# Per-token maxima of an adapter moved from a double PSUM bank to a ring of single banks, in two-head pieces

## What is computed

```python
end_pos = encoder_hidden_states.shape[1] - NUM_TOKENS        # 508 keys, 4 tokens
enc, ca = encoder_hidden_states[:, :end_pos], encoder_hidden_states[:, end_pos:]
hs = _mha(hidden_states @ Wq, enc @ Wk, enc @ Wv)            # 8 heads of 20
ca_q1 = jnp.einsum('btc,th->bch', ca, Wq_ca)                 # 96 queries
ca_q1 = ca_q1[:, indices, :]                                 # spread over the 256 rows
ca_hs1 = _mha(ca_q1, residual, residual)                     # the token scores
ca_hs2 = _mha(ca_hs1 @ Wq, ca @ Wk_ca, ca @ Wv_ca)
out = (hs + ca_hs2) @ Wout + b_out + residual
```

## Time and profile before

| | us |
|---|---|
| median of 3 runs | 1375.84 (1375.4 to 1378.92) |
| the profiled execution | 1376.87 |
| its span in the trace | 1375.0 |
| TensorE busy | 1272.2 (93%) |
| VectorE busy | 963.3 (70%) |
| GpSimd busy | 810.6 (59%) |
| ScalarE busy | 779.5 (57%) |

### The profile page before, as it was taken

How to read it: one execution, slowest core, us unless ns; L and a number is a source line. 1 busy time by engine, 2 the same in 40 slices (tenths; PEclk the granted TensorE clock), 3 DMA queues, 4 the chain that set the end, 5 groups by cost and what they waited for, 6 DMA issues and landing times. The chain is left out here.

```text
span 1375.0 us, 39629 instructions
## 1 busy us (share of the span) xinstructions
PE 1272.2 (93%) x16812; PEld 1084.5 (79%) x16812; DVE 963.3 (70%) x1758; ACT 779.5 (57%) x1420; POOL 810.6 (59%) x866
## 2 busy tenths in 40 slices
PE   4889999976999999999889999999999999999597
PEld 3677777755989989899757888888888888887597
DVE  4677887734777777777457767686867676765584
ACT  2366666644656665665346656565656665655364
POOL 2278887657645655555426656566656565667364
PEclk9999999957999999999969999999999999999798
DMA  6001110002000000000010000000010000000000
GB/s 133 21 11 50 50 35 2 2 7 65 2 2 2 2 3 2 2 2 2 1 42 8 2 8 2 8 2 8 1 49 2 2 2 2 2 2 2 13 15 25
DMA packets 31992, 20.40 MB, mean 15 GB/s; under 512 B 21415, under 2 KB 30347, under 8 KB 31819
## 3 DMA queue, kind: packets, MB, share of 16 engines
q1 hardware_dynamic: 31819, 17.88, 5.2%
HBM read 16.56 MB, written 1.31 MB: 13 GB/s over the span
## 5 line engine op out<-in xcount | busy, mean ns | idle before, releaser
L530 POOL TENSOR_TENSOR cross_probs_l<-cross_probs 128x1024 f16<-128x1024 f32 x160 | 302.6, 1893 | 54.6 <-ACT cross_probs L614 54.6
L614 ACT ACTIVATE cross_probs<-cross_score 128x1024 f32<-128x1024 f32 x160 | 163.9, 1024 | 189.4 <-PE cross_score L844 189.4
L698 DVE TENSOR_REDUCE cross_top<-cross_max 128x2 f32<-128x1024 f32 x160 | 195.7, 1223 | 63.6 <-PE cross_max L818 63.6
L1618 POOL TENSOR_TENSOR ad_probs_l<-ad_probs 128x1024 f16<-128x1024 f32 x64 | 120.8, 1893 | 91.2 <-ACT ad_probs L1692 90.8
L530 POOL TENSOR_TENSOR self_probs_l<-self_probs 128x1024 f16<-128x1024 f32 x80 | 151.4, 1892 | 1.2 <-ACT self_probs L614 1.2
L864 PEld LDWEIGHTS cross_pv<-cross_v_h,cross_probs 128*128 128x128 bf16 x1280 | 117.1, 98 | 38.0 <-issue 26.8
L614 ACT ACTIVATE self_probs<-self_score 128x1024 f32<-128x1024 f32 x80 | 81.9, 1024 | 110.9 <-PE self_score L844 110.8
L864 PE MATMUL cross_pv<-cross_v_h,cross_probs 128*128 128x65 bf16 x1280 | 135.7, 196 | 6.1 <-POOL cross_probs_l L530 5.3
L865 PE MATMUL cross_pv<-cross_v_l,cross_probs 128*128 128x64 f16 x1280 | 134.4, 194 | 0.0
L866 PE MATMUL cross_pv<-cross_v_h,cross_probs_l 128*128 128x65 bf16 x1280 | 134.0, 194 | 0.0
L844 PE MATMUL cross_score<-cross_qk_h 64*128 64x256 f32 x640 | 120.5, 373 | 0.0
(11 more groups left out here) (438 smaller groups left out, 4792.4 us busy)
## 6 DMA issues: line engine op xcount, KB each, us to landing
ad_ctx_rows<-in_ctx SPq DMA_DIRECT2D x8, 192.0 KB, 2.8
cross_ctx_rows<-in_ctx SPq DMA_DIRECT2D x8, 192.0 KB, 2.6
sw_raw<-in_L_xattn_wq SPq DMA_DIRECT2D x2, 640.0 KB, 6.1
sw_raw<-in_L_xattn_wk SPq DMA_DIRECT2D x2, 640.0 KB, 4.8
sw_raw<-in_L_xattn_wv SPq DMA_DIRECT2D x2, 640.0 KB, 5.2
cw_raw<-in_L_xattn_wq SPq DMA_DIRECT2D x2, 640.0 KB, 4.2
lr_raw<-in_L_xattn_w_ff SPq DMA_DIRECT2D x2, 640.0 KB
out<-x_rows SPq DMA_DIRECT2D x8, 160.0 KB, 1.9
```

The source lines that it names most:

```text
L530: nc.gpsimd.tensor_tensor(probs_l[:, n % PR, :, :].rearrange("p j k -> p (j k)"), whole, whole.bitcast(BF16)[:, 1::2], ALU.subtract).then_ ...
L614: nc.scalar.activation(probs[:, n % PR, :, :].rearrange("p j k -> p (j k)"), score_bank[:, :], ACT.Exp, scale=SCALE).then_inc(exped, 1)
L698: nc.vector.reduce_max(out, scores, AX.X).then_inc(max_read, 1)
L1618: nc.gpsimd.tensor_tensor(probs_l[:, n % PR, :, :].rearrange("p j k -> p (j k)"), whole, whole.bitcast(BF16)[:, 1::2], ALU.subtract).then_ ...
```

## The change

The maxima of the token scores (`top`) go through the shared banks. A group is two heads instead of four: 2 x 256 columns fill one bank. Four groups of a batch stand in pairs at the ends of the slots `4b+1` and `4b+2`, and VectorE reduces each with one instruction of 512 columns. `top` now has its place in the ring, so a batch has four more entries and the banks of all later entries are dealt out anew. The two semaphores of their own go. Besides, `qs`, the token scores, stand behind the second half of weigh in the step instead of before it.

```diff
         add(1, "xv", 4)
+        if (p := pair(g, WEIGH)) is not None:
+            out += [(1, ("weigh", p, group)) for group in (2, 3)]
         add(1, "qs", 4, 0)
         add(1, "qs", 5, 1)
-        if (p := pair(g, WEIGH)) is not None:
-            out += [(1, ("weigh", p, group)) for group in (2, 3)]
-        add(1, "top", 1, 0)
-        add(1, "top", 2, 1)
+        for n in range(4):
+            add(1, "top", 1 + n // 2, n)
         add(1, "rows", 0)
...
-    ELSEWHERE = ("weigh", "top", "qs", "s2", "p2", "xv")
+    ELSEWHERE = ("weigh", "qs", "s2", "p2", "xv")
...
                             _, b, n = key
-                            dve.wait_ge(top_filled, b * 2 + n + 1)
-                            nc.vector.reduce_max(top_q[:, CDIM + 4 * n:CDIM + 4 * n + 4],
-                                                 max_bank[0:CDIM, :].rearrange("p (h k) -> p h k", h=4), AX.X).then_inc(top_read, 1)
+                            dve.wait_ge(filled, order.filled(key))
+                            nc.vector.reduce_max(top_q[:, CDIM + 2 * n:CDIM + 2 * n + 2],
+                                                 shared[order.bank(key)][0:CDIM, :].rearrange("p (h k) -> p h k", h=2), AX.X).then_inc(emptied, 1)
...
                 elif what == "mq":
-                    pe.wait_ge(top_read, b * 2 + 2)
+                    pe.wait_ge(emptied, order.read(("top", b, 3)))
...
                     pe.wait_ge(emptied, order.read(("k", p)))
-                    after(pe, top_read, extra_fills(g, 1))
                 after(pe, max_read, p * ROUNDS + step)
...
-            def top(g, b, n):
+            def top(b, n):
 
                 j = b % 2
                 if n == 0:
                     pe.wait_ge(emptied, order.read(("rows", b)))
                     pe.wait_ge(cm_ready, b + 1)
-                after(pe, top_read, b * 2 + n)
-                after(pe, max_read, issued(g, MAX))
-                for h in range(4):
-                    mm = nc.tensor.matmul(max_bank[0:CDIM, h * SEQ:(h + 1) * SEQ], c_m[j][0:3 * HT, 4 * n + h, :],
+                bank_ = claim(("top", b, n))
+                for h in two:
+                    mm = nc.tensor.matmul(bank_[0:CDIM, h * SEQ:(h + 1) * SEQ], c_m[j][0:3 * HT, 2 * n + h, :],
                                           r_s[j][0:3 * HT, :], start=True, stop=True)
-                mm.then_inc(top_filled, 1)
+                mm.then_inc(filled, 1)
```

## The result

| | before | after |
|---|---|---|
| median of 20 runs each, us | 1377.38 | 1372.03 |
| ratio, 95% interval | | 0.9958 (0.9941 to 0.9975) |
| profiled execution, us | 1376.87 | 1368.42 |
| its span, us | 1375.0 | 1366.6 |

The change makes the kernel faster, by 5.8 us as the ratio has it (3.4 to 8.1). The ratio leaves out one slow run on each side, 1591.92 us before and 1389.86 us after. The forecast was 10.8 us: the sign and the range of 1357 to 1374 us were right, the size was about double. The time also lies outside the 1361 to 1371 us that the forecast gave to its own case. The profiled execution does not show where the missing half went: its adapter is 10.9 us shorter (last value matmul at 289.46 us for 300.34), close to the 11.4 that the sum gave.

The account below looks back on a forecast made before the run. TensorE, busy 93% of the span, was taken as the bound, with idle time and half clock in the adapter. Start 2.1, six batches 3.6, last batch 3.0, tail 1.2 + 1.5 sum to 11.4 us: forecast 1365 us, range 1357 to 1374.

Parts of the forecast that it names:

- its own case: The forecast's main case for the whole kernel: 1365 us, within 1361 to 1371 us, chance 0.50.
- (g): Clock in six steady batches: one in three falls after the x wait, 1.5 us worse; 0.6 us each, 3.6 us.
- (f): Last batch: no x in slot 30, so no new wait; 3.7 us if the clock stays up, 3.0 taken.
- (h): Tail: with slot 32's wait halved, the clock falls later or not at all; 1.5 us, between 0 and 6.
- (d): Token scores behind the values: shorter waits for ScalarE's exponential of the scores; 1.2 us from slots 32 and 33.
- (a): Top leaves the double bank: in slot 17 find_max goes at 162.35 us instead of 163.72.
- (b): VectorE's maximum split into two of 512 columns: +0.07 to +0.15 us a pair, 1.1 to 2.4 us in all.
- (c): Slots 17 and 18: VectorE is late next, TensorE waits 1.2 to 1.4 us at x; 1.1 us gained for the batch.
- (e): Start: slots 2 and 3 lose waits of 1.41 and 1.36 us, less the split pair; 2.1 us gained.
- slower rival: Falls after x last twice as long, costing each of six batches 2.1 us: 1386 us, chance 0.07.
- rival with a fall in every batch: The clock's fall merely moves to uncovered work in every batch: 2.4 us gained, about 1374 us, chance 0.15.

Follow-up runs that it names:

- x_first: Kernel after, with x ahead of mt in the ring and mt behind the first half of weigh: 1361.92 us, 0.9878 of the kernel before.
- only_top: Kernel after, with the token scores put back ahead of the values, so only the maxima move: 1365.54 us, 0.9921 of the kernel before.
- only_qs: Kernel before, with only the token scores moved behind the values, the maxima left in the double bank: 1379.35 us, 1.002 of the kernel before.
- before_b: Kernel before, no edit, executed for its second profile: span 1376.7 us.
- the last version: Kernel after, with x ahead of mt and the token scores back ahead of the values: 1360.91 us (0.9876), later 1357.84 us (0.9869).
- after_b: Kernel after, no edit, executed again for its third profile: median 1370.12 us, 0.9945 of the kernel before, span 1380.0 us.
- after_d: Kernel after, no edit, executed for its fifth profile: span 1362.1 us.

## Where the prediction was right, and the steps that failed

The step that failed is the clock, in (g) and with it in (f) and (h); (d) failed besides. The waits of (a), (b) and (c) came out nearly as forecast. The marks that split the adapter are the first value matmul, the first `ot` transposes of slots 9, 29 and 33, and the last value matmul. In us gained, five columns against the first profile of before, and last the mean of the five profiles after against the mean of the three before:

| term | forecast | after, 1 | after, 2 | after, 3 | after, 4 | after, 5 | means |
|---|---|---|---|---|---|---|---|
| start (e) | 2.1 | 2.8 | 2.9 | -0.9 | 3.1 | 2.3 | 3.3 |
| first steady batch | 0.6 | 2.8 | 2.8 | 2.8 | 2.8 | 2.8 | 1.7 |
| next five (g) | 3.0 | 5.7 | 1.8 | -9.2 | 5.7 | 0.2 | 1.2 |
| last batch (f) | 3.0 | -0.4 | 3.4 | 4.2 | -1.2 | 4.2 | 0.3 |
| tail (d, h) | 2.7 | 0.0 | 0.0 | 1.5 | 0.0 | 1.2 | 0.5 |
| sum | 11.4 | 10.9 | 10.9 | -1.7 | 10.4 | 10.7 | 7.0 |

(a) and (b) were right for `find_max`, which follows at once, and for the split pair, 1.28 us. The split costs 0.07 us a pair, the lower bound of the sum and under the 0.125 us of its estimate. But `top` 1 is "about to issue when its bank comes free" in slot 17 and not in every batch; in slots 9, 21 and 25 it waits 0.6 us for the reading of q, which the sum had at nothing. The prediction had named this wait as a sign of being wrong. Its share was not measured by itself either.

(c) was right: VectorE is next, the wait at `x` is 1.1 to 1.25 us, and a batch without a fall is 1.0 to 1.2 us shorter than one of before with its short fall. x_first shows it from the other side: with the bank of `x` free earlier, VectorE's 1.2 us of idle and 0.8 us of the batch go. I missed the new wait of `qw` for k, 0.37 us; its share was not measured by itself.

(d) was wrong by its 1.2 us. The guard was in the text, that the exponential of the token scores has only 0.2 us to spare, but it was read off slot 17, where the token scores do not wait. In slots 32 and 33 they wait for ScalarE in either order, and their exponential starts 0.62 us behind them in both kernels (slot 32). The values no longer stand between it and the next scores to cover it: these wait 0.44 us with `find_max` in between, and 0.95 us behind slot 33, where there is no `find_max`. only_top and only_qs say the same: the move brings nothing that can be measured.

(h) had 1.5 us, and the profiles have none in three cases and 1.5 and 1.2 us in two. The clock of the tail was down from 268 us on with the wait halved, as from 277 us before; in the third and fifth profile it fell 7 to 8 us behind the start of the token scores of slot 32 (289.2 and 275.9 us), not 1 to 2 us as in the first two, and those are the ones that gained.

(f) was read off one profile. Its 3.0 us rest mostly on the fall of 6.8 us in slot 30, and the other two profiles of before have none there: their last batch took 28.3 us, for 31.0 in the first. The profiles after have 26.8 to 32.2 us, with a fall in two of five. On average the term is 0.3 us.

The start and the first batch gave 2.3 us more than forecast, by the means. The -0.9 in the third profile is the clock too. It was down from 33 us on for 30.7 us there, and for 20.5 us in the first; before_b has the same, with 34.1 us and its first value matmul at 69.6 us instead of 65.8.

What the forecast lacked most is in (g). I took one batch in three with a fall, and there are nine falls in the thirty batches of the five profiles. I priced a fall at 1.5 us. Six of the nine are short and cost 0.2 to 1.4 us each, 1.0 on average. But a fall of this kernel can also last 13.7 or 23.9 us, at 3.3 or 7.5 us each: there are three such, 18.3 us together, 3.7 us an execution. The mean fall cost 2.7 us, not 1.5. The slower rival had this mechanism, with falls of twice the length; it asked for them in most batches, and two long ones were enough. The median, 1372.0 us, lies where the rival with a fall in every batch was put (1371.5 to 1376), but that is luck for the rival: 21 of the thirty batches have no fall.

How far this explains the time is less sure, since one profile of the five holds 15.0 of the 18.3 us, and the other four end the adapter within 0.6 us of each other wherever the falls lie, the one with the fall of 13.7 us included. Taken over all groups the medians are 1369.2 us for 42 runs after and 1377.8 us for 72 before (without the one of 1591.92), 8.6 us apart, and the means 6.8 us; the mean spans of the profiles are 7.8 us apart. The 20 runs of the first comparison had 5.4 by their medians. So these means explain the step from 10.8 to some 7, and chance between groups of runs may hold the rest; the intervals of the three groups overlap between 0.9941 and 0.9961. The mean granted clock on record for each of the 42 runs points the same way. It is 0.960 on average in the ten runs below 1367 us, 0.954 in the sixteen from 1370 to 1377 and 0.945 in the four above, and 0.937 in the slowest, 1389.86 us. But it moves by about 0.01 with how much of the start was recorded, and it does not tell one long fall from several short ones. Whether the runs at 1372 to 1376 us, of which there are many, are those with one long fall is open: none of them was profiled.

Nor is it settled what makes a fall long. For the wait at `x`: the two of 23.9 us begin 2.2 and 2.1 us behind the start of `x`, and four profiles of kernels with the wait gone or halved have no fall over 3.4 us in their steady batches. The 12 runs of the last version also lie closer (standard deviation 3.1 us, 5.6 in 42 of the kernel after, 3.3 in 72 before), but the six of x_first do not (4.7 us). Against it: in the fifth profile a fall that begins 2.1 us behind the `x` of slot 10 lasts only 3.4 us, and its fall of 13.7 us begins before `x`, behind a wait of 0.56 us; the last batch, which has no `x`, had one of 13.7 us in the first profile and a longer one in the fourth; and short falls come without any wait at `x`. Four profiles are few. What the three long falls in the steady batches share is that they begin in a slot `4b+2`, ahead of its projections, and run on through the projections, where the other engines are idle a third of the time and more. Short falls begin there too, so the place alone does not make them long.

The version with the token scores where they were and `x` ahead of `mt` beats both kernels: 17 to 18 us under the kernel before and about 9 under the change.

## What to carry to other kernels

When a wait of TensorE is removed, follow the next engine to the next bank that is read late: the wait may come back a few entries on, and moving one entry in the ring took it away here and brought some 8 us more, about as much as the change itself. Ask too what a fall of the clock costs at each place: from one execution to the next the same kernel lost nothing, 3.3 or 15 us of its steady batches to long falls. The same holds of the kernel before: a term read off a fall that its one profile happens to have, as (f) was, is mispriced. So one profile can hold the whole gain and miss the loss; take three or more before a few microseconds in a thousand are put down to a cause.

## What the runs showed of the hardware

TensorE stayed at 1.2 GHz for 23.9 us twice in the middle of the adapter while it was busy 23.60 of 23.60 and 23.90 of 23.90 us by the windows of after_b. In other executions of the same kernel the same instructions ran at 2.4 GHz, or had it back after 3.4 us. Being busy, as the profile counts it, was not enough to get the clock back. The Trainium skill, page "TensorE: Matmul & The Clock Gate", section "What's actually happening", says that the full clock returns once TensorE has been kept busy; the short falls agree with that, the two long ones do not, and here the measurement decides.

A long wait was not needed to lose it either. In x_first a fall came behind 3.3 us in which TensorE was busy 2.92 us with 79 mostly small matmuls, and in after_d behind a wait of 0.56 us.
```profile
105.00:108.30 3.30, 2.92 (x79) 2.64 (x80) 2.63 (x6) 1.89 (x3) 3.22 (x3) 0.99 0.00 0
108.30:112.00 3.70, 3.70 (x44) 3.24 (x40) 2.48 (x6) 2.49 (x6) 3.62 (x3) 0.55 0.07 16
```
